# An attention kernel's turned probabilities moved as one tile in place of two halves, and its rank step put earlier on VectorE

## The reference

```python
xn = layernorm(x)
q, k, v = xn @ W_q.T + b_q, xn @ W_k.T + b_k, xn @ W_v.T + b_v
z = (q @ k.T) / sqrt(512) * adj                 # adj: 2048 x 2048, zeros and ones
z = where(z == 0, -10000, z)
x = x + relu(softmax(z, axis=1) @ v)
X = layernorm(x)
w, idx = top_k(softmax(X @ Wr), 2); w = softmax(w)
x = x + swiglu(X, shared) + sum over the two experts of w * swiglu(X, expert)
```

## Time and profile before

| | |
|---|---|
| median of 3 runs | 1401.52 us (1401.38 to 1402.24) |
| the profiled execution | 1403.48 us |
| its span | 1401.8 us |
| TensorE matmul busy | 1372.9 us, 98% of the span |
| VectorE busy | 908.3 us, 65% |
| ScalarE busy | 453.4 us, 32% |
| GpSimd busy | 191.0 us, 14% |
| mean granted clock of TensorE | 0.994 |

### The profile page before, as it was taken

One profiled execution on the slowest core, in us unless ns is written; L12 is line 12 of the kernel. 1 busy time (PEld: TensorE's weight loads), 2 busy tenths in 40 slices (PEclk: granted clock), 3 DMA queues, 4 the chain that ended last, 5 costly groups with the idle time before them and its releaser, 6 DMA issues.

```text
span 1401.8 us, 19781 instructions
## 1 busy us (share of the span) xinstructions
PE 1372.9 (98%) x6720; PEld 1181.9 (84%) x6720; DVE 908.3 (65%) x1957; ACT 453.4 (32%) x702; POOL 191.0 (14%) x234
## 2 busy tenths in 40 slices
PE   9998999999999999999999999999999999999998
PEld 7887887787787878898898989898898989888887
DVE  7956766766676666646575747657375745367874
ACT  4522212121122134434242514324242424243331
POOL 3500011112111223021102010100101020200000
PEclk9999999999999999999999999999999999999999
DMA  5806467546644587164435225261354444453101
GB/s 183 251 26 185 126 176 182 139 127 188 177 145 127 164 248 255 62 161 136 120 110 158 83 46 203 39 200 33 65 175 87 147 110 139 126 167 105 46 16 60
DMA packets 114420, 185.47 MB, mean 132 GB/s; under 512 B 13776, under 2 KB 47568, under 8 KB 114336
## 3 DMA queue, kind: packets, MB, share of 16 engines
q1 hardware_dynamic: 98064, 153.43, 35.4%
q0 software_dynamic: 9760, 18.93, 7.2%
q10 hardware_dynamic: 6528, 12.22, 3.1%
HBM read 129.82 MB, written 55.77 MB: 132 GB/s over the span
## 4 chain that ended last, share of the span: by engine, by line
PE 64%; DVE 1%; DMA 1%; issue 1%; POOL 0%; ACT 0%; DVEq 0%; POOLq 0%
PE bank L305 58%; PE bank L1035 5%; PE bank L1026 1%; DMA owners<-owner,idx 1%; DVE z L1898 0%; PE bank L987 0%; PE bank L867 0%; POOL slots L683 0%; PE bank L845 0%; PE bank L861 0%; DVE pT_l L1450 0%; DVE fill L1594 0%; POOL owners L685 0%; DVE sc L1586 0%; DVE hT_l L1450 0%
## 5 line engine op out<-in xcount | busy, mean ns | idle before, releaser
L1823 DVE TENSOR_TENSOR hid<-bank,hid 128x384 f32<-128x384 f32 (+1 forms) x80 | 46.8, 585 | 176.0 <-PE bank L305 175.8
L305 PE MATMUL bank<-dn_h,hT_h 128*128 128x512 f32 x320 | 125.7, 393 | 0.2 <-DVE hT_l L1450 0.2
L305 PE MATMUL bank<-dn_h,hT_l 128*128 128x512 f32 x320 | 125.8, 393 | 0.0
L305 PE MATMUL bank<-dn_l,hT_h 128*128 128x512 f32 x320 | 125.5, 392 | 0.0
L305 PE MATMUL bank<-xq_h,gate_h 128*128 128x384 f32 (+1 forms) x320 | 111.3, 348 | 0.1
L305 PE MATMUL bank<-xq_h,gate_l 128*128 128x384 f32 (+1 forms) x320 | 111.2, 347 | 0.0
L305 PE MATMUL bank<-xq_l,gate_h 128*128 128x384 f32 (+1 forms) x320 | 110.8, 346 | 0.0
L305 PE MATMUL bank<-xq_h,up_h 128*128 128x384 f32 (+1 forms) x320 | 110.7, 346 | 0.0
L305 PE MATMUL bank<-xq_h,up_l 128*128 128x384 f32 (+1 forms) x320 | 110.4, 345 | 0.0
L305 PE MATMUL bank<-xq_l,up_h 128*128 128x384 f32 (+1 forms) x320 | 110.4, 345 | 0.0
L1121 ACT ACTIVATE hT_h<-hid 128x384 fp32r<-128x384 f32 (+1 forms) x96 | 53.8, 561 | 164.2 <-DVE hid L1823 124.7
(11 more groups left out here) (277 smaller groups left out, 3294.3 us busy)
## 6 DMA issues: line engine op xcount, KB each, us to landing
sc<-in_adj_dram SPq DMA_DIRECT2D x32, 512.0 KB, 7.1
gate_raw<-in_L_ffn_Wg_dram SPq DMA_DIRECT2D x16, 1024.0 KB, 5.5
up_raw<-in_L_ffn_Wu_dram SPq DMA_DIRECT2D x16, 1024.0 KB, 10.1
dn_raw<-in_L_ffn_Wd_dram SPq DMA_DIRECT2D x16, 1024.0 KB, 12.6
p_moved<-turned SPq DMA_DIRECT2D x30, 512.0 KB, 7.5
turned<-p_moved SPq DMA_DIRECT2D x120, 128.0 KB, 4.7
x_t<-in_x_dram SPq DMA_DIRECT2D x24, 256.0 KB, 5.0
slots<-x2row ACTq DMA_DIRECT2D x12, 512.0 KB, 4.4
```

The source lines that it names most:

```text
L305: mm = pe.matmul(o, lhs(a, c), rhs(b, c), start=first and n == 1, stop=last and n == 3 * len(chunks))
L1823: dve.tensor_tensor(hid[:, c % 2, 0:w], bank[2 + c % 2][:, 0:w], hid[:, c % 2, 0:w], ALU.mult).then_inc(sem("hid"), 1)
```

## The change

The turned probabilities of a tile are laid out as one block, so that each run between two partitions is 2 KB long in place of 1 KB. One write of 1 MB and four reads of 256 KB take the place of two writes and eight reads. The write waits for both halves of turn_squares; the load of the first half of the adjacency rows stands ahead of it and no longer behind a write. Both `high` wait for all four reads. On VectorE `ranks` stands right behind the second mask, and in step 0 the two `low` stand between the fills as in the other steps.

```diff
-    p_moved = nc.dram_tensor("p_moved", [2, P, BANKS * HALF * Q], F32, kind="Internal").ap()
+    p_moved = nc.dram_tensor("p_moved", [P, BANKS * NT * Q], F32, kind="Internal").ap()
-        turned = at("turned", 176 * K, [P, 2, BANKS, HALF * Q])
+        turned = at("turned", 176 * K, [P, BANKS, NT * Q])
         def moved_half(h):
-            return turned[:, h, :, :].rearrange("p i (k q) -> p k i q", q=Q)
+            return turned[:].rearrange("p i (k q) -> p k i q", q=Q)[:, HALF * h:HALF * h + HALF, :, :]
@@ move
                 for h in range(2):
                     sp.wait_ge(sem("p_turned"), 2 * i + h + 1)
-                    sp.dma_start(p_moved[h, :, :], turned[:, h, :, :].rearrange("p a f -> p (a f)")).then_inc(sem(f"p_half{h}"), 16)
+                    if h == 1:
+                        sp.dma_start(p_moved, turned[:].rearrange("p a f -> p (a f)")).then_inc(sem("p_moved"), 16)
                     load_adj(i + 1, h)
-                for h in range(2):
-                    sp.wait_ge(sem(f"p_half{h}"), MOVED * i + 16)
-                    by_bank = p_moved[h, :, :].rearrange("(i r) (a f) -> a r i f", i=BANKS, a=BANKS)
-                    for a in range(BANKS):
-                        sp.dma_start(turned[Q * a:Q * a + Q, h, :, :], by_bank[a]).then_inc(sem(f"p_half{h}"), 16)
+                sp.wait_ge(sem("p_moved"), MOVED * i + 16)
+                by_bank = p_moved.rearrange("(i r) (a f) -> a r i f", i=BANKS, a=BANKS)
+                for a in range(BANKS):
+                    sp.dma_start(turned[Q * a:Q * a + Q, :, :], by_bank[a]).then_inc(sem("p_moved"), 16)
@@ ScalarE, high
-                act.wait_ge(sem(f"p_half{h}"), MOVED * (i + 1))
+                act.wait_ge(sem("p_moved"), MOVED * (i + 1))
@@ VectorE, turn_squares
-                    dve.transpose(turned[:, h, :, :].rearrange("p a (k q) -> p k a q", q=Q),
+                    dve.transpose(moved_half(h),
@@ VectorE, attention_step
                 mask(i + 1, 1 - b, 1)
+                if counted:
+
+                    ranks(i - 1)
                 fill_zeros(i + 1, 1 - b, 0)
-                if prev:
-                    low(i, 0)
+                low(i, 0)
                 fill_zeros(i + 1, 1 - b, 1)
                 mask(i + 1, 1 - b, 2)
-                if prev:
-                    low(i, 1)
+                low(i, 1)
...
                 if prev:
                     logits(i)
-                else:
-
-                    low(i, 0)
-                    low(i, 1)
-                if counted:
-                    ranks(i - 1)
```

## The result

The changed kernel takes 1433.93 us (median of 4 runs, 1432.67 to 1437.32), beside 1401.88 us for the kernel before on the same chip: a ratio of 1.0222 (95% interval 1.0188 to 1.0256), some 32 us slower. The forecast was slower by 8.1 us, with 1417 us as its far end. The direction held, the size did not. The profiled execution took 1433.76 us; its span of 1432.1 us is 30.3 us longer than before, and the mean granted clock is 0.985 in place of 0.994.

A forecast was written before the change was run, and what follows sets the result against it. TensorE, busy 98% of the span, bounds the kernel; 21.9 us hang on x2row. Loop waits +2.4 (19.2 against 16.8), first steps +5.7, clock unchanged: +8.1 on the 1401.52 us median gives 1409.6 us, range 1393 to 1417.

The forecast's parts named there:

- The mechanism: Attention's even steps: rstd no longer waits for the scatter; TensorE waits before L867 (route_logits) for x2T, 2 to 4 us each.
- The clock: TensorE at half clock behind waits: 5.1 us lost today, kept unchanged because waits have the same size and place.
- all six +5.1: Upper end of the clock term: all six even-step waits bring a lower-clock stretch, 5.1 us more than today.
- The reads' term: Move of the probabilities: 6.4 us from the reads' issue to the first copy, between 5.0 and 6.9.
- The write's term: Move of the probabilities: the whole write lands 6.4 us after its issue, between 5.8 and 7.5.
- L: Time from the first write's issue to ScalarE's first pT_h: 13.3 us today, 13.9 forecast, between 11.9 and 15.5.
- The ranks' price: VectorE, odd steps: ranks behind the second mask make exponentials, turn_squares and the write 1.2 us later.
- P: Start of an odd step on TensorE; forecast write at P + 20.2, x2T at P + 35.7, TensorE ready at P + 32.5.
- The first steps: Written-out steps 0, 1 and 2: later by 0.9, 2.9 and 1.9 us, together +5.7, between -1 and +9.
- The early landing: Rival: reads run at 376 GB/s or fixed times hide, L 12.0, 1390 us; chance 0.20.
- the balance: Rival: L near 13.0, as today's first half, waits 2.3 us, 1401.5 us; chance 0.14.
- the ranks do nothing: Rival: something else holds the earlier scatter, the old wait stays, near 1408 us; chance 0.03.

The follow-up runs named there:

- Variant 3: Changed kernel with x2T (keep_turned) ahead of the first copy, high(i, 0), in ScalarE's order: 1399.47 us, ratio 0.9979 to the kernel before.
- variant 11: Changed kernel with the next load of x and the store of the sum held until the reads have landed: 1427.51 us, ratio 1.0163 to the kernel before.
- Variant 7: Changed kernel with 12 unused matmuls of 512 columns ahead of route_logits in even steps: 1420.41 us, ratio 1.0084 to the kernel before.
- variant 1: Kernel before with only the ranks moved behind the second mask, halves kept: 1385.38 us, ratio 0.9875 to the kernel before.
- variant 2: Changed kernel with ranks back at their old place behind the logits, so the whole tile alone: 1434.63 us, ratio 1.023 to the kernel before.
- variant 8: Kernel before with ranks behind the second mask and each copy waiting for the reads of both halves: 1407.33 us, ratio 0.9985 to the kernel before.

## Why the prediction was right or wrong

**The mechanism was right.** x2row's wait goes, rstd waits for var_e alone, TensorE stands before L867 eight times for x2T (2.7 to 4.1 us each), step 1 for the first time. Variant 3 shows that this order on ScalarE is the cause of these waits. The longer run brought no faster rate, as forecast: 188 to 245 GB/s in variant 11, against 226 with 1 KB.

**The clock was the step that failed.** The forecast's reason, "waits of the same size in the same place, so I keep 5.1 us", put the change at 0, and it was +13.7 us. In the kernel before three of the six waits for x2row brought a stretch at the lower clock, of 3.4 us each, and the longest, 3.4 us in step 4, brought none. In the changed kernel the six are 3.1 to 4.1 us long with 0.2 to 0.8 us before them at x2row, and all six brought one, three of them 6.8 us long; steps 1 and 2 brought one each as well, which the forecast gave no clock term at all. Its own upper bound, "all six +5.1", left out that a stretch can last twice as long and that the new waits of the first steps have the same effect. Variant 7 confirms the term by taking most of it away. The stated range did not hold even the forecast's own upper ends together: 12.0 in the loop, 9 in the first steps and 5.1 of clock on 1401.5 are 1427.6 us, where the range ended at 1417.

**The reads' term was mis-sized:** 6.4 us forecast, with 6.9 as its upper end; 7.9 in step 12, and 7.5 to 8.7 over all steps. The upper end was 4.6 us of data and 2.3 of fixed time. Variant 11 has 4.6 us between a slow start of 1.8 and a quiet end of 1.1, so 2.9 in place of 2.3 around the data, and the load and the store behind the reads, which the forecast had left out, add 0.5: 8.0. **The write's term** was too long: 6.4 forecast, 5.4 to 6.1 measured, and 6.7 once, in step 2; the scatter had gone. Together L is 14.8 in place of 13.9, inside its bounds of 11.9 to 15.5.

**The ranks' price** was 1.2 us forecast: the first transfer went out at P + 20.58 where 20.2 was said. x2T at P + 36.8 where 35.7 was said. In the even steps from 4 to 14 this makes 21.9 us of waiting at L867 and 3.8 at x2row, 25.7 in place of 19.2: **+8.9 against +2.4**.

**The first steps:** step 0 +2.4, and 0.6 for yT_l, where +0.9 was forecast (its own L was 14.8, not the 13.3 that went into it, again by the reads' term, 8.1 us); step 1 +3.3 against +2.9; step 2 +1.8 against +1.9. Together +8.1 against +5.7.

In sum: 17.0 us of waits where 8.1 was forecast, and 13.7 of clock where 0 was. Misses of 0.9 us in L and 0.4 us in the ranks' price became 9 us in the waits, since they are paid in steps 0, 1 and 2 and in each even step from 4 to 14.

**The rivals.** The early landing and the balance fall with L. That the ranks do nothing falls with variant 1, and is true in a way that the forecast did not think of: beside the whole tile, variant 2 gives the same time without them.

What stays open: why reads into all partitions stay under 280 GB/s, why some waits bring a stretch of 3.4 us at the lower clock and others of 6.8, and why the kernel before stood at two levels in different sessions.

## What to carry to other kernels

Joining two transfers joins their completions: before doing it, look at what else stands behind the first one in the waiting engine's order, and move that ahead, as 34 us of 1434 hung here on one small copy. The late landing itself cost another 15 us by way of VectorE, which variant 3's order on ScalarE does not take away. Where TensorE is nearly always busy, price a new wait as the wait plus what the clock takes afterwards, and use the worst stretch that the trace shows, not the mean of what the old waits did. And try the parts of a change alone: one of the two here was worth 1.25%, and the other hid it.

## What the hardware showed that was not expected

- Waits of 2.7 to 4.1 us before route_logits took two thirds as much again in the clock (27.9 us of waits before L867, eight stretches of 37.6 us at half the clock behind them, a loss of 18.8). In variant 8 waits of 1.7 to 2.1 us there were followed by such a stretch in six of seven steps. Filling 2.9 us of each wait with empty matmuls gave back 14.3 us of span, though x2T came no sooner.
- A scatter of four indirect DMAs beside the move cost the move 2.7 us (L 13.2 against 10.4), more than any other single thing but the wait for the second half. Beside the whole tile it cost 1.6 us (16.4 against 14.8).
- Reads into all 128 partitions, in runs of 2 KB, ran at 260 to 270 GB/s behind a write to DRAM, the load and the store behind them included, where loads of weights in runs of 1 KB into as many partitions ran at 376.
- Four reads of 256 KB take 1.6 to 1.8 us from the first issue to the full rate, and in the last 1.1 us before the waiting engine goes on they move 0.01 MB.
